# Two tiny VectorE instructions take scalar operands, and ScalarE copies the values at another point of each step

## The chip, the cores and the metric

The kernel runs on one core of a Trainium2 chip. The metric is the device time of one execution in microseconds (us), as the median of several runs. The engines are TensorE (PE, with its weight load PEld), VectorE (DVE), ScalarE (ACT), GpSimd (POOL) and SyncE (SP), which here issues DMAs.

## The reference

One perceiver layer over 8 batches of 128 tokens with 512 features, with a context of 2048 rows of 384 features for each batch. It is a cross-attention, a self-attention (softmax over the queries, causal) and a feed-forward part with rounding to small floats, each behind a layer norm:

```
x = x + _L0_xattn_ref(_layernorm(x, axis=-1), ctx_768, ...)
x = x + _L0_attn_ref(_layernorm(x, axis=-1), ...)
x = x + _L0_ffn_ref(_layernorm(x, axis=-1), ...)
```

The change concerns the cross-attention, which takes some four fifths of the time:

```
q = (x @ Wq).reshape(B, Nq, HEADS, DIM_HEAD)
k = (context @ Wk).reshape(B, context.shape[1], HEADS, DIM_HEAD)
v = (context @ Wv).reshape(B, context.shape[1], HEADS, DIM_HEAD)
sim = jnp.einsum('bihd,bjhd->bhij', q, k) * SCALE
attn = jax.nn.softmax(sim, axis=-1)
out = jnp.einsum('bhij,bjhd->bihd', attn, v)
```

## The kernel before

Every fp32 operand of a product is split into a high and a low fp16 half, and a product is made of three passes (high by high, low by high, high by low). The cross-attention is a loop over 128 slots, 16 for each batch. A slot is one head of one of four head pairs over one half of the context (1024 columns). In the first 8 slots of a batch stands the first half of the context, in the other 8 the second. `behind(s)` is true for these latter ones: there the running maximum, the sums and the weighted values of the first half are merged with the new ones.

All engines follow one hand-written schedule. Each has a function `steady(s)` that is called for s = 0 to 127, and the orders of the engines are tied together by semaphores alone. In step s:

- TensorE makes the values of slot s+1 (`value_tiles`, 18 matmuls into the one bank `v_ps`), the keys of slot s (`key_quarter`, 9 matmuls into the one bank `k_ps`), the weighted values of slot s-5 (`weighted_values`, into `o_ps`), and in even steps the scores of two slots (`scores`, 12 matmuls into `e_ps`). It may not refill `v_ps` before VectorE has made the low half of the values that stand there (`v_low`, semaphore `v_split`), nor `k_ps` before `k_low` (`k_split`), nor `e_ps` before ScalarE's second exponential of the slots there (`p_full`).
- ScalarE works three slots behind (x = s-3). `slot_bias` turns a maximum into the bias of the exponential. `exps_high` writes the exponentials in fp16 (`p_h`), `exps_full` writes them once more in fp32 and sums them (`p_f`, `p_sum`), `v_high` and `k_high` copy values and keys out of their banks as fp16, `fade_of` makes the factor by which the first half's results shrink, and `ctx_high` (every fourth step) casts a new piece of context. In an odd step x is the first slot of a pair, and both biases of the pair are made in this step.
- VectorE takes in odd steps the two maxima of the pair (`slot_maximum`, `q_max`, 128x1024 to 128x1). In slots with `behind` each is followed by `new_max`, the minimum of two columns of `q_max` (the maxima are kept negated). Then come `add_sums` (`o_den`, one column) and `accumulate` (`acc`), `o_reciprocal`, `v_low` and `k_low`.
- GpSimd makes the low half of the exponentials (`p_low`, tile `p_l`), the low half of the context (`ctx_low`, tile `ctx_l`, every fourth step, in steps 2, 6, 10 and 14 of a batch), and the normalised outputs.
- SyncE issues the DMAs that transpose `p_h` and `p_l` into `pt_h` and `pt_l`.

From slot 112 on GpSimd and VectorE also split the weights of the next stage (lines L2040 and L1578). Rows of the trace name a line: L670 is inside `three_passes`, which both the value and the key products use, L739 the scores, L759 and L761 the weighted values, L1158 `v_high`, L1166 `k_high`, L1173 `slot_bias`, L1195 `exps_high`, L1202 `exps_full`, L1523 `v_low`, L1530 `k_low`, L1537 and L1542 the two instructions of `slot_maximum`, L1554 `acc`, L1566 `o_den`, L1969 `ctx_low`.

Of the kernel before, what the change touches and what calls it, by code (L numbers as in the profile page):

```python
# [8 lines left out]
ALU = mybir.AluOpType  # L9
# [26 lines left out]
SLOTS = B * PAIRS * QUARTERS  # L36
# [24 lines left out]
def perceiver_kernel(nc, x, ctx_t, xwq, xwk, xwv, xwo, xbo, awq, abq, awk, abk, awv, abv,  # L61
# [136 lines left out]
    with ExitStack() as ctx:  # L198
# [3 lines left out]
        def sem(name):  # L202
            return ctx.enter_context(nc.semaphore(name))
# [58 lines left out]
        o_rec_ready = sem("o_rec_ready")  # L262
# [76 lines left out]
        def slot_of(s):  # L339
            return s // PER_BATCH, s % PER_BATCH // PER_HALF, s % PER_HALF // 2, s % 2  # L340
# [9 lines left out]
        def v_tiles_of(s):  # L350

            return s // PER_BATCH, s % PER_HALF // 4, s % PER_BATCH // PER_HALF * PER_HALF + 2 * (s % 4)

        def behind(s):
            return s % PER_BATCH >= PER_HALF
# [36 lines left out]
        def v_bank(s):  # L392
            return o_ps[0] if s == 1 else v_ps
# [694 lines left out]
        def _(act):  # L1088
# [29 lines left out]
            def x_norm(r):  # L1118
                act.wait_ge(rstd_ready, 3)
                act.wait_ge(shift_ready, 2)  # L1120
                act.activation(x_in[:, r, :], x_in[:, r, :], ACT.Identity, scale=rstd[:, r:r + 1],
                               bias=shift[:, r - 4:r - 3]).then_inc(xn_ready, 1)


            def x_high(r):
                act.wait_ge(xn_ready, r + 1)
                if r == 4:
                    act.wait_ge(wq_split, DCH)
                act.activation(xn_half[:, r - 4, 0, :], x_in[:, r, :], ACT.Copy).then_inc(xt_hi, 1)
# [17 lines left out]
            def v_high(s):  # L1147

                b, g, j0 = v_tiles_of(s)
                act.wait_ge(v_filled, s + 1)  # L1150
                if b and s % 4 == 0:

                    act.wait_ge(pv_done, s - PER_BATCH + 4)
                if s == PER_HALF:
                    act.wait_ge(wv_split, 2)
                elif s == PER_HALF + 4:
                    act.wait_ge(wk_split, PAIRS)
                act.activation(v[g][:, j0:j0 + 2, :, 0:DH], v_bank(s)[:, :].rearrange("p (j h d) -> p j h d", j=2, d=DH),  # L1158
                               ACT.Copy).then_inc(v_hi, 1)

            def k_high(s):
                u, i = s // 2, s % 2
                act.wait_ge(k_filled, s + 1)
                if u >= K_RING:
                    act.wait_ge(e_filled, u - K_RING + 1)
                act.activation(k_h[:, u % K_RING, i * QW:i * QW + QW], k_ps[:, :], ACT.Copy).then_inc(k_hi, 1)  # L1166

            def slot_bias(s):

                col = s % PER_BATCH  # L1170
                act.wait_ge(e_maxed, s + 1)
                top = new_max if behind(s) else q_max
                act.activation(bias[:, col:col + 1], top[:, col:col + 1], ACT.Identity, scale=EXP_SCALE, bias=SHIFT)\  # L1173
                    .then_inc(bias_ready, 1)

            def fade_of(s):

                col, old = s % PER_BATCH, s % PER_BATCH - PER_HALF
                act.wait_ge(bias_ready, s + 1)
                if s >= PER_BATCH:  # L1180
                    b, _, p, h = slot_of(s)
                    act.wait_ge(o_rec_ready, 3 * (PAIRS * (b - 1) + p) + h + 1)
                act.activation(fade[:, col:col + 1], bias[:, old:old + 1], ACT.Exp, scale=-1.0, bias=bias[:, col:col + 1])\
                    .then_inc(fade_ready, 1)

            def exps_high(s):

                col = s % PER_BATCH
                act.wait_ge(bias_ready, s + 1)
                if s == 0:  # L1190

                    act.wait_ge(xt_split, B)
                if s >= H_RING:
                    act.wait_ge(pt_h_landed[(s - H_RING) % T_RING], 16 * ((s - H_RING) // T_RING) + 16)
                act.activation(p_h[:, s % H_RING, :, :], e_ps[s % 2][:, :, :], ACT.Exp, scale=EXP_SCALE,  # L1195
                               bias=bias[:, col:col + 1]).then_inc(p_hi, 1)

            def exps_full(s):
                col = s % PER_BATCH
                if s >= F_RING:  # L1200
                    act.wait_ge(p_split, s - F_RING + 1)
                act.activation(p_f[:, s % F_RING, :, :], e_ps[s % 2][:, :, :], ACT.Exp, scale=EXP_SCALE,  # L1202
                               bias=bias[:, col:col + 1], accum_out=p_sum[:, col:col + 1]).then_inc(p_full, 1)
# [40 lines left out]
            def steady(s):  # L1244
                x = s - X_LAG
                ahead, pair = 0 <= x < SLOTS, s % 2 == 1
                if x == 0:

                    slot_bias(0)
                    v_high(s + 1)  # L1250
                    exps_high(0)
                    slot_bias(1)
                    k_high(s)
                    exps_full(0)
                    return
                if ahead:
                    if pair:
                        slot_bias(x)
                    exps_high(x)
                    if pair:  # L1260
                        slot_bias(x + 1)
                if 0 < s and s + 1 < SLOTS:
                    v_high(s + 1)
                if s == 2:
                    x_norm(7)
                    for r in (6, 7):
                        x_high(r)
                if ahead:
                    exps_full(x)
                if 0 < s < SLOTS:  # L1270
                    k_high(s)
                if ahead and behind(x):
                    fade_of(x)

            for s in range(SLOTS):
                steady(s)
                for i in QUERIES_BEHIND.get(s, ()):
                    q_high(i)
                if s == 1:
                    wv_high(1)  # L1280
                    x_norm(6)
                if s in ctx_behind:
                    ctx_high(ctx_behind[s])
                if s in load_behind:
                    load_ctx(load_behind[s])

                if 0 <= s - SLOTS + 19 < 2 * CC:
                    load_weight(s - SLOTS + 19)
                if 2 * CC <= s - SLOTS + 20 < 16:
                    load_weight(s - SLOTS + 20)  # L1290
                if s in LOAD_X:
                    load_x(LOAD_X[s])
# [67 lines left out]
            def weights_high(b, name):  # L1360
# [9 lines left out]
                else:  # L1370
# [3 lines left out]
                               scale=weight_scale(name)).then_inc(ws_hi, 1)  # L1374

            steady(SLOTS)
            slot_bias(SLOTS - 2)
            exps_high(SLOTS - 2)
# [88 lines left out]
        def _(dve):  # L1467
# [65 lines left out]
            def slot_maximum(s):  # L1533

                col, old = s % PER_BATCH, s % PER_BATCH - PER_HALF
                dve.wait_ge(e_filled, s // 2 + 1)
                ins = dve.tensor_reduce(q_max[:, col:col + 1], e_ps[s % 2][:, :, :].rearrange("p i n -> p (i n)"), AX, ALU.max,  # L1537
                                        negate=True)
                if behind(s):
                    ins.then_inc(e_reduced, 1)  # L1540
                    dve.wait_ge(e_reduced, s // PER_BATCH * PER_HALF + s % PER_HALF + 1)
                    ins = dve.tensor_tensor(new_max[:, col:col + 1], q_max[:, col:col + 1], q_max[:, old:old + 1], ALU.min)  # L1542
                ins.then_inc(e_maxed, 1)

            def accumulate(s):
# [15 lines left out]
            def add_sums(s):  # L1561
                b, _, p, h = slot_of(s)
                col, old = s % PER_BATCH, s % PER_BATCH - PER_HALF
                dve.wait_ge(p_full, s + 1)
                dve.wait_ge(fade_ready, PER_HALF * b + s % PER_HALF + 1)
                dve.scalar_tensor_tensor(o_den[:, p, h, :], p_sum[:, old:old + 1], fade[:, col:col + 1], p_sum[:, col:col + 1],  # L1566
                                         ALU.mult, ALU.add).then_inc(o_rec_ready, 1)

            def o_reciprocal(n):
                dve.wait_ge(o_rec_ready, 3 * n + 2)  # L1570
# [570 lines left out]
```

## Time and profile before

| | |
|---|---|
| median of 3 runs | 948.62 us (947.88 to 949.03) |
| the profiled execution, its own time | 949.72 us |
| its span in the trace | 947.7 us |
| granted TensorE clock, mean | 0.996 of full speed |
| TensorE busy | 908.3 us, 96% |
| VectorE busy | 600.1 us, 63% |
| ScalarE busy | 575.4 us, 61% |
| GpSimd busy | 506.7 us, 53% |

The span runs from the first to the last record of the execution, and the execution's own time is 2 us more. Busy time says how long an engine held an instruction. An instruction that waits inside the engine, after it has been started, counts as busy too. A row of the timeline gives the start, the duration, the engine, the line, the operation, what it writes and reads, how many like it are merged in the row (x3), and in brackets how long the engine had been idle before it and who released it.

### The profile page before, as it was taken

The numbers are of one execution on the slowest core, as the hardware profiler recorded it, in microseconds if no ns is written. First come the engines' busy times: TensorE is split into PE (matmuls) and PEld (weight loads), VectorE is DVE, ScalarE is ACT, GpSimd is POOL, SyncE is SP. The second block draws the span as 40 slices with busy tenths as digits, with TensorE's granted clock in tenths as the row PEclk, the third lists the DMA queues.
The fourth block names the chain that finished last, engine by engine and source line by source line (L and its number), as shares of the span: only waits on it lengthen the run. The fifth ranks groups of instructions, "written<-read, shape, count | busy, mean of one in ns | idle before, by whom it ended". The sixth has DMA issues, their size and how long they took to land.

```text
span 947.7 us, 19492 instructions
## 1 busy us (share of the span) xinstructions
PE 908.3 (96%) x7470; PEld 566.4 (60%) x7470; DVE 600.1 (63%) x973; ACT 575.4 (61%) x1014; POOL 506.7 (53%) x393
## 2 busy tenths in 40 slices
PE   6999999999999999999999999988999899999998
PEld 4556666666666666666666666655666455544444
DVE  6645665566556656665665566566866668886634
ACT  4856676666766776666677666756666522336540
POOL 4646466456545755675466556766876766310000
PEclk9999999999999999999999999999999999999999
DMA  9366566656656576565666656866798663133502
GB/s 332 89 153 149 123 136 140 154 130 134 145 123 129 129 146 132 122 138 133 123 140 154 142 123 151 186 122 129 158 183 177 113 105 96 39 107 78 178 12 79
DMA packets 340268, 126.35 MB, mean 133 GB/s; under 512 B 316113, under 2 KB 317905, under 8 KB 340177
## 3 DMA queue, kind: packets, MB, share of 16 engines
q1 hardware_dynamic: 324832, 95.87, 48.8%
q10 hardware_dynamic: 15344, 29.23, 10.3%
q8 instruction: 61, 1.00, 0.5%
q14 instruction: 31, 0.25, 0.1%
HBM read 45.36 MB, written 2.10 MB: 50 GB/s over the span
## 4 chain that ended last, share of the span: by engine, by line
PE 86%; DVE 6%; ACT 4%; issue 1%; DMA 1%; SPq 1%; POOL 0%; ACTq 0%; DVEq 0%
PE v_ps L670 26%; PE k_ps L670 24%; PE e_ps L739 9%; PE e_ps L670 8%; PE o_ps L759 5%; PE e_ps L1021 3%; PE o_ps L761 3%; DVE new_max L1542 2%; PE o_ps L776 2%; DVE q_max L1537 2%; PE o_ps L1014 1%; ACT p_h L1195 1%; PE e_ps L1014 1%; DVE v L1523 1%; ACT v L1158 1%
## 5 line engine op out<-in xcount | busy, mean ns | idle before, releaser
L1979 POOL TENSOR_TENSOR p_l<-p_f,p_h 128x1024 f16<-128x1024 f32 x128 | 273.0, 2133 | 260.7 <-ACT p_f L1202 259.9
L1537 DVE TENSOR_REDUCE q_max<-e_ps 128x1 f32<-128x1024 f32 x128 | 153.4, 1219 | 49.6 <-PE e_ps L739 49.6
L1530 DVE TENSOR_TENSOR k_l<-k_ps,k_h 128x512 f16<-128x512 f32 x128 | 88.5, 692 | 125.4 <-ACT k_h L1166 125.4
L670 PE MATMUL v_ps<-wv_h,ctx_h 128*128 128x256 f16 x756 | 124.7, 274 | 24.3 <-DVE v L1523 24.3
L1195 ACT ACTIVATE p_h<-e_ps,bias 128x1024 f16<-128x1024 f32 x128 | 143.2, 1119 | 2.4 <-issue 0.3
L1523 DVE TENSOR_TENSOR v<-v_ps,v 128x512 f16<-128x512 f32 x127 | 87.6, 690 | 88.6 <-ACT v L1158 87.9
L1202 ACT ACTIVATE p_f<-e_ps,bias 128x1024 f32<-128x1024 f32 x128 | 142.0, 1109 | 0.0
L670 PE MATMUL v_ps<-wv_l,ctx_h 128*128 128x256 f16 x756 | 124.2, 273 | 0.0
L670 PE MATMUL v_ps<-wv_h,ctx_l 128*128 128x256 f16 x756 | 124.1, 273 | 0.0
L759 PE MATMUL o_ps<-v,pt_h 128*128 128x128 f16 x1024 | 104.2, 220 | 0.6 <-DVE acc L1554 0.6
L670 PE MATMUL k_ps<-ctx_h,wk_h 128*128 128x512 f16 x384 | 104.4, 381 | 0.0
L670 PE MATMUL k_ps<-ctx_h,wk_l 128*128 128x512 f16 x384 | 103.8, 379 | 0.0
L670 PE MATMUL k_ps<-ctx_l,wk_h 128*128 128x512 f16 x384 | 103.8, 379 | 0.0
L1969 POOL TENSOR_TENSOR ctx_l<-raw,ctx_h 128x1536 f16<-128x1536 f32 x31 | 96.0, 3098 | 13.5 <-ACT ctx_h L1145 12.5
L761 PE MATMUL o_ps<-v,pt_l 128*128 128x64 f16 x1024 | 100.8, 193 | 0.0
L670 PEld LDWEIGHTS v_ps<-wv_h,ctx_h 128*128 128x128 f16 x756 | 64.7, 98 | 59.3 <-issue 52.9
L759 PEld LDWEIGHTS o_ps<-v,pt_h 128*128 128x128 f16 x1024 | 90.3, 98 | 15.7 <-issue 0.7
L1158 ACT ACTIVATE v<-v_ps 128x512 f16<-128x512 f32 x127 | 74.9, 590 | 38.8 <-PE v_ps L670 37.1
L761 PEld LDWEIGHTS o_ps<-v,pt_l 128*128 128x128 f16 x1024 | 88.6, 98 | 15.0
L1166 ACT ACTIVATE k_h<-k_ps 128x512 f16<-128x512 f32 x128 | 76.5, 598 | 16.9 <-PE k_ps L670 16.7
L670 PEld LDWEIGHTS v_ps<-wv_l,ctx_h 128*128 128x128 f16 x756 | 74.1, 98 | 8.7
L670 PEld LDWEIGHTS v_ps<-wv_h,ctx_l 128*128 128x128 f16 x756 | 74.1, 98 | 8.7
(311 smaller groups left out, 1336.9 us busy)
## 6 DMA issues: line engine op xcount, KB each, us to landing
raw<-in_ctx_t ACTq DMA_DIRECT2D x27, 768.0 KB, 5.4
w_raw<-in_w_t SPq DMA_DIRECT2D x32, 256.0 KB, 4.0
raw<-in_ctx_t SPq DMA_DIRECT2D x4, 768.0 KB, 7.3
pt_h<-p_h SPq DMA_TRANSPOSE x128, 2.9
pt_l<-p_l SPq DMA_TRANSPOSE x128, 2.8
out<-xr SPq DMA_DIRECT2D x7, 256.0 KB, 2.0
x_in<-in_x SPq DMA_DIRECT2D x6, 256.0 KB, 8.5
o_all<-in_x ACTq DMA_DIRECT2D x6, 256.0 KB, 3.7
```

Of the source, the lines that this page charges most:

```text
L670: mm = pe.matmul(acc, a(c), m(c), start=(i == 0), stop=(i == len(todo) - 1))
L739: mm = pe.matmul(e_ps[h][:, i, :], left[rows, p, tokens], right[rows, u % K_RING, cols], start=first, stop=last)
L759: pe.matmul(acc_bank[:, 0:VW], pt_h[:, s % T_RING, j, :], v[g][:, tile, head, :], start=(j == 0), stop=False, skip_group_check=True)
L761: mm = pe.matmul(acc_bank[:, 0:DH], pt_l[:, s % T_RING, j, :], v[g][:, tile, head, 0:DH], start=False, stop=(j == 2 * JT - 1), skip_group_ ...
L1158: act.activation(v[g][:, j0:j0 + 2, :, 0:DH], v_bank(s)[:, :].rearrange("p (j h d) -> p j h d", j=2, d=DH), ACT.Copy).then_inc(v_hi, 1)
L1195: act.activation(p_h[:, s % H_RING, :, :], e_ps[s % 2][:, :, :], ACT.Exp, scale=EXP_SCALE, bias=bias[:, col:col + 1]).then_inc(p_hi, 1)
L1202: act.activation(p_f[:, s % F_RING, :, :], e_ps[s % 2][:, :, :], ACT.Exp, scale=EXP_SCALE, bias=bias[:, col:col + 1], accum_out=p_sum[:, c ...
L1523: dve.tensor_tensor(v[g][:, j0:j0 + 2, :, DH:VW], v_bank(s)[:, :].rearrange("p (j h d) -> p j h d", j=2, d=DH), v[g][:, j0:j0 + 2, :, 0:DH ...
L1530: dve.tensor_tensor(k_l[:, s // 2 % K_RING, cols], k_ps[:, :], k_h[:, s // 2 % K_RING, cols], ALU.subtract)\
L1537: ins = dve.tensor_reduce(q_max[:, col:col + 1], e_ps[s % 2][:, :, :].rearrange("p i n -> p (i n)"), AX, ALU.max, negate=True)
L1969: pool.tensor_tensor(ctx_l[b % 2][:, q, :, :], raw[:, i % 2, :, :], ctx_h[b % 2][:, q, :, :], ALU.subtract).then_inc(ctx_split, 1)
L1979: pool.tensor_tensor(p_l[:, s % L_RING, :, :], p_f[:, s % F_RING, :, :], p_h[:, s % H_RING, :, :], ALU.subtract).then_inc(p_split, 1)
```

## The change

There are two parts. The first rewrites two instructions of VectorE that work on one column of 128 partitions. `new_max` was a `tensor_tensor` with two one-column tensor inputs; it becomes a `tensor_scalar` with one tensor input and one per-partition scalar operand. `o_den` was a `scalar_tensor_tensor` with two tensor inputs and a scalar; it becomes a `tensor_scalar` with one tensor input and two scalar operands. The second moves ScalarE's copy of the values, `v_high(s + 1)`: in odd steps from behind the second bias to the very front, in even steps from between the two exponentials to behind both.

```diff
                 if ahead:
-                    if pair:
-                        slot_bias(x)
-                    exps_high(x)
-                    if pair:
-                        slot_bias(x + 1)
-                if 0 < s and s + 1 < SLOTS:
-                    v_high(s + 1)
+                if ahead and not pair:
+                    exps_high(x)
                 if s == 2:
                     x_norm(7)
                     for r in (6, 7):
                         x_high(r)
-                if ahead:
+                if ahead and not pair:
+                    exps_full(x)
+                if 0 < s and s + 1 < SLOTS:
+                    v_high(s + 1)
+                if ahead and pair:
+                    slot_bias(x)
+                    exps_high(x)
+                    slot_bias(x + 1)
                     exps_full(x)
                 if 0 < s < SLOTS:
                     k_high(s)
...
-                    ins = dve.tensor_tensor(new_max[:, col:col + 1], q_max[:, col:col + 1], q_max[:, old:old + 1], ALU.min)
+                    ins = dve.tensor_scalar(new_max[:, col:col + 1], q_max[:, col:col + 1], q_max[:, old:old + 1], None, ALU.min)
...
-                dve.scalar_tensor_tensor(o_den[:, p, h, :], p_sum[:, old:old + 1], fade[:, col:col + 1], p_sum[:, col:col + 1],
-                                         ALU.mult, ALU.add).then_inc(o_rec_ready, 1)
+                dve.tensor_scalar(o_den[:, p, h, :], p_sum[:, old:old + 1], fade[:, col:col + 1], p_sum[:, col:col + 1],
+                                  ALU.mult, ALU.add).then_inc(o_rec_ready, 1)
```

ScalarE's order in one odd and the following even step of the first batch (s = 9 and 10; `bias` is `slot_bias`, `p_h` and `p_f` the two exponentials, `v_102` the values). Before:

```order
L1173 ACTIVATE bias<-q_max 128x1
L1195 ACTIVATE p_h<-e_ps,bias 128x1024
L1173 ACTIVATE bias<-q_max 128x1
L1158 ACTIVATE v_102<-v_ps 128x8x64
L1202 ACTIVATE p_f,p_sum<-e_ps,bias 128x1024
L1166 ACTIVATE k_h<-k_ps 128x512
L1195 ACTIVATE p_h<-e_ps,bias 128x1024
L1158 ACTIVATE v_102<-v_ps 128x8x64
L1202 ACTIVATE p_f,p_sum<-e_ps,bias 128x1024
L1166 ACTIVATE k_h<-k_ps 128x512
```

and with the change:

```order
L1158 ACTIVATE v_102<-v_ps 128x8x64
L1173 ACTIVATE bias<-q_max 128x1
L1195 ACTIVATE p_h<-e_ps,bias 128x1024
L1173 ACTIVATE bias<-q_max 128x1
L1202 ACTIVATE p_f,p_sum<-e_ps,bias 128x1024
L1166 ACTIVATE k_h<-k_ps 128x512
L1195 ACTIVATE p_h<-e_ps,bias 128x1024
L1202 ACTIVATE p_f,p_sum<-e_ps,bias 128x1024
L1158 ACTIVATE v_102<-v_ps 128x8x64
L1166 ACTIVATE k_h<-k_ps 128x512
```

In the odd step the values are now copied before the biases, so everything down to the copy of the keys stands one copy later behind them; in the even step the second exponential stands ahead of the copy.

In step 2 the same statement order also lets the normalisation of the last rows of x pass the copy. ScalarE before:

```order
L1145 ACTIVATE ctx_h_86<-raw 128x1536
L1158 ACTIVATE v_102<-v_ps 128x8x64
L1121 ACTIVATE x_in<-x_in,shift,rstd 128x512
L1129 ACTIVATE xn_half<-x_in 128x512 x2
L1166 ACTIVATE k_h<-k_ps 128x512
```

and with the change:

```order
L1145 ACTIVATE ctx_h_86<-raw 128x1536
L1121 ACTIVATE x_in<-x_in,shift,rstd 128x512
L1129 ACTIVATE xn_half<-x_in 128x512 x2
L1158 ACTIVATE v_102<-v_ps 128x8x64
L1166 ACTIVATE k_h<-k_ps 128x512
```

Here three small instructions moved ahead of the copy. On VectorE nothing changes its place; only the kind of the two instructions does, as in this odd step with `behind` (s = 15), before:

```order
L1537 TENSOR_REDUCE q_max<-e_ps 128x1
L1542 TENSOR_TENSOR new_max<-q_max 128x1
L1537 TENSOR_REDUCE q_max<-e_ps 128x1
L1542 TENSOR_TENSOR new_max<-q_max 128x1
L1566 SCALAR_TENSOR_TENSOR o_den<-p_sum,fade 128x1
L1554 SCALAR_TENSOR_TENSOR acc<-acc,fade,o_ps 128x128
```

and with the change:

```order
L1538 TENSOR_REDUCE q_max<-e_ps 128x1
L1543 TENSOR_SCALAR new_max<-q_max 128x1
L1538 TENSOR_REDUCE q_max<-e_ps 128x1
L1543 TENSOR_SCALAR new_max<-q_max 128x1
L1567 TENSOR_SCALAR o_den<-p_sum,fade 128x1
L1555 SCALAR_TENSOR_TENSOR acc<-acc,fade,o_ps 128x128
```

The line numbers are one higher there because the changed `steady` of ScalarE is one line longer.

## Rows read from the trace of the kernel before

**Rows 1.** The page, busy time by engine.

```profile
PE 908.3 (96%) x7470; PEld 566.4 (60%) x7470; DVE 600.1 (63%) x973; ACT 575.4 (61%) x1014; POOL 506.7 (53%) x393
```

**Rows 2.** Waits of PE: waited for, us in total, times, longest.

```profile
PE v_ps L670 <- DVE v L1523: 24.3, 17, 2.4
```

**Rows 3.** Timeline of PE, 290 to 314 us, starts of value products.

```profile
290.85 0.50 PE L670 MATMUL v_ps<-wv_h,ctx_h 128*128 128x256 f16 x3
...
297.13 0.49 PE L670 MATMUL v_ps<-wv_h,ctx_h 128*128 128x256 f16 x3 [1.52 <-DVE v L1523]
...
303.21 0.50 PE L670 MATMUL v_ps<-wv_h,ctx_h 128*128 128x256 f16 x3
...
307.81 0.49 PE L670 MATMUL v_ps<-wv_h,ctx_h 128*128 128x256 f16 x3
...
313.89 0.50 PE L670 MATMUL v_ps<-wv_h,ctx_h 128*128 128x256 f16 x3
```

**Rows 4.** Timeline of DVE, around 292 us and around 628 us.

```profile
292.21 1.99 DVE L1542 TENSOR_TENSOR new_max<-q_max 128x1 f32<-128x1 f32 x1
...
296.29 0.69 DVE L1523 TENSOR_TENSOR v<-v_ps,v 128x512 f16<-128x512 f32 x1 [0.28 <-ACT v L1158]
...
628.90 0.69 DVE L1523 TENSOR_TENSOR v<-v_ps,v 128x512 f16<-128x512 f32 x1 [0.54 <-ACT v L1158]
```

**Rows 5.** Timeline of POOL, around 291 us.

```profile
291.10 3.10 POOL L1969 TENSOR_TENSOR ctx_l<-raw,ctx_h 128x1536 f16<-128x1536 f32 x1 [0.27 <-ACT ctx_h L1145]
```

**Rows 6.** DVE instructions of L1542 and L1566: duration ns minimum/median/maximum.

```profile
L1542 DVE TENSOR_TENSOR new_max<-q_max x64: 158/160/2909, 92.1 to 749.5; 128x1 f32<-128x1 f32 x64
...
L1566 DVE SCALAR_TENSOR_TENSOR o_den<-p_sum,fade x64: 208/982/1102, 108.7 to 766.5; 128x1 f32<-128x1 f32 x64
```

**Rows 7.** Chain that ended last: value products of steps 7, 112 and 125.

```profile
69.40 2.07 PE v_ps L670 x18
...
654.46 3.17 PE v_ps L670 x18
...
726.38 2.07 PE v_ps L670 x18
```

**Rows 8.** Windows: busy time by engine, granted clock, DMA share, GB/s.

```profile
652.00:662.00 10.00, 7.56 (x56) 4.57 (x55) 5.34 (x11) 6.83 (x13) 6.13 (x7) 0.83 0.51 117
```

**Rows 9.** DVE tensor_scalar, the POOL instructions beside it, and acc.

```profile
777.00 1.15 POOL L2084 TENSOR_TENSOR n_half<-o_all,n_half 128x512 f16<-128x512 f32 x1
777.03 1.41 DVE L1652 TENSOR_SCALAR o_all<-xr,mean_var,rstd 128x512 f32<-128x512 f32 x1 [0.27 <-POOL rstd L1959]
...
797.44 1.45 POOL L2075 TENSOR_TENSOR xr<-xr,o_all 128x512 f32<-128x512 f32 x1
...
798.53 0.39 DVE L1699 TENSOR_SCALAR c_col<-c_sum,s_col 128x4 f32<-128x4 f32 x1
...
L1699 DVE TENSOR_SCALAR c_col<-c_sum,s_col x2: 229/310/390, 798.5 to 824.6; 128x4 f32<-128x4 f32 x2
```

**Rows 10.** Timeline of ACT, 309 to 319 us; DVE at 318.80.

```profile
309.97 0.60 ACT L1158 ACTIVATE v<-v_ps 128x512 f16<-128x512 f32 x1 [0.42 <-PE v_ps L670]
...
315.26 0.20 ACT L1173 ACTIVATE bias<-q_max 128x1 f32<-128x1 f32 x1 [1.20 <-DVE q_max L1537]
315.50 1.11 ACT L1195 ACTIVATE p_h<-e_ps,bias 128x1024 f16<-128x1024 f32 x1
...
316.60 0.59 ACT L1158 ACTIVATE v<-v_ps 128x512 f16<-128x512 f32 x1
317.08 1.12 ACT L1202 ACTIVATE p_f<-e_ps,bias 128x1024 f32<-128x1024 f32 x1
...
318.17 0.61 ACT L1166 ACTIVATE k_h<-k_ps 128x512 f16<-128x512 f32 x1
...
318.80 0.69 DVE L1530 TENSOR_TENSOR k_l<-k_ps,k_h 128x512 f16<-128x512 f32 x1 [0.62 <-ACT k_h L1166]
```

**Rows 11.** Timeline of PE, 303 to 310 us: keys of an even step.

```profile
309.77 0.59 PE L670 MATMUL k_ps<-ctx_h,wk_h 128*128 128x512 f16 x2
```

More of the change, by code:

```diff
@@ L1267, in steady @@
                         x_high(r)
-                if ahead:
+                if ahead and not pair:
[6 more added lines that the diff above has]
+                    slot_bias(x + 1)
                     exps_full(x)
```

## The prediction

> **What bounds the kernel now.** I read the page first: TensorE is busy for 908.3 of 947.7 us, far more than any other engine [rows 1], so only what shortens TensorE's work or its idle time (39.4 us) can count. The waits of TensorE come next. One line holds most of the idle time: 24.3 us in 17 waits of the value products on VectorE's `v_low` [rows 2]. Then the timeline of TensorE shows how regular the loop is. An odd and an even step together, a pair, take 313.89 - 303.21 = 10.68 us when nothing is late, and 303.21 - 290.85 = 12.36 us when the even step's value products wait, 1.52 us here [rows 3]. Nothing else in the loop is late: in a regular pair every engine but TensorE has idle time, and TensorE none.
>
> How much of this is there in all? From step 7 to step 125 lie 59 pairs, and the chain that ended last puts them at 726.38 - 69.40 = 656.98 us [rows 7]. At 10.68 us each they would take 630.12 us. So 26.9 us are lost in the loop. Between 652 and 662 us, behind the longest of the waits, the clock too was down: a mean of 0.83 was granted [rows 8], a mixture of 2.4 and 1.2 GHz, and one group of 18 value matmuls took 3.17 us where others take 2.07 [rows 7]. That is in the 26.9 us and goes if the wait in front of it goes.
>
> Why is `v_low` late? VectorE's order in an odd step is maximum, `new_max`, maximum, `new_max`, sums, `v_low`. `new_max` handles one column and takes 160 ns in the median, but up to 2909 [rows 6]. The one at 292.21 took 1.99 us and ended at 294.20 [rows 4]. GpSimd's `ctx_low` ran from 291.10 to 294.20 [rows 5]: the tiny instruction ended the moment the big one did. I find this in 15 of the 64 `new_max`, 14 of them behind `ctx_low` and one behind an addition of the bias row, and 15 of the 17 waits follow them (the two others lie in the opening steps). `o_den` has the same sickness, 982 ns in the median where 208 are possible [rows 6], but there `v_low` is not late behind it.
>
> Both have two tensor inputs in SBUF. That is what the Trainium skill says of such a pair (SBUF — State Buffer, Who interferes with whom): a VectorE instruction with two SBUF inputs shares a read interface with a GpSimd instruction that reads SBUF, and the later one waits for the whole of the other. By that rule, the trace agrees.
>
> **Part one, scalar operands.** After the change each has one tensor input. If that takes it out of GpSimd's way, `new_max` falls to some 0.21 us (I take the shortest `o_den`, which has a scalar operand [rows 6]) and all 15 waits go: 26.9 us, the difference to the regular pair. The other 49 become 0.05 us longer each, two in a pair, hidden: in the stalled step the whole of VectorE's chain was 1.5 us late, in a regular one `v_low` only waits for ScalarE's copy. `o_den` gives nothing, for it was on no path.
>
> No row shows a one-column `tensor_scalar` on VectorE, so the price is bounded from both sides. Lower end: free, as above, minus 26.9. Upper end: it waits as before, and part one gives 0. There are rows on the wide form. `o_all` (128x512, two scalar operands) began at 777.03, beside a GpSimd instruction that ran from 777.00 to 778.15, and took 1.41 us; `c_col` (128x4) took 390 ns and ended at 798.92 with a GpSimd instruction that ended at 798.89, while its other execution took 229 [rows 9]. So `tensor_scalar` as such isn't free of this wait. What is left is whether one column is. I think rather yes: the waiting forms stream several columns, and a single one can't be split between two paths.
>
> The Trainium skill has the rule behind the wide form (VectorE: DVE Perf Modes, Mode 2×_2P): a one-input operation that stays in SBUF is read over both ports if the outermost non-unit dimension is even; one column has no such dimension, and the text leaves it open. Read strictly the rule frees `new_max` and the sum is the same as mine; read as "equal counts are enough" it doesn't, and that is the second rival.
>
> **Part two, the order on ScalarE.** In odd steps the copy goes to the front. The values are there 309.97 - 307.81 = 2.16 us after their products begin [rows 3, 10]. From there all times are counted from the start of the odd step's value products. Copy to bias 0.48 (316.60 to 317.08), bias to `exps_high` 0.24 (315.26 to 315.50), on to `exps_full` 1.10 (315.50 to 316.60, the second bias in it), to `k_high` 1.09 (317.08 to 318.17), to `k_low` 0.63 (to 318.80), its length 0.69, and 0.15 until TensorE starts, as from the end of `v_low` at 296.98 to 297.13 [rows 3, 4, 10]. The sum is 6.54 us. TensorE wants the bank for the next keys at 309.77 - 303.21 = 6.56 us [rows 3, 11]. Before, the same chain ended at 318.80 + 0.69 + 0.15 - 313.89 = 5.75 us [rows 3, 10]. So the move eats a reserve of 0.81 us down to 0.02. This is the only place where it can hurt in every pair, and there are 61 of them: each 0.1 us beyond costs 6.1 us. I take 0.025 us a pair, 1.5 us in all. In the even step the copy of the values falls 1.4 us later, about where TensorE has its keys ready anyway; `v_low` still ends over 1 us before the next odd step needs the bank, and `exps_full`, which frees `e_ps`, starts no later than before. I cost this at nothing. If the first kind of wait stays, moving the copy does help: `v_low` no longer waits for it, 0.28 or 0.54 us in the stalled steps [rows 4].
>
> In step 2 the copy stands behind three small instructions, some 1.7 us. TensorE's step 3 starts about 1 us later, but its step 4 waited some 1.5 us for VectorE anyway (one of the two opening waits), so I count 0.2 us.
>
> **Sum.** Minus 26.9, plus 1.5, plus 0.2 is -25.2 us. The profiled execution took 949.72 us (span 947.7), 1.1 above the median of 948.62, and what is removed is the same in both. From the median: **923.4 us**.
>
> **The rivals.**
> - *Free column, but the order costs.* The chain above comes out 0.1 to 0.3 us longer than 6.54, and TensorE waits for `k_low` in each pair: 6 to 18 us, giving 928 to 940. For it: a reserve of 0.02 is less than I can read. Against: each link is measured back to back.
> - *One column waits like four.* `new_max` stretches as before, and only the copy's place helps: 15 waits shorter by 0.41 on the mean of 0.28 and 0.54, 6.2 us, less 1.7: 944.1. For it: `c_col` [rows 9]. Against: a column can't be halved.
> - *Slower.* `new_max` still waits, and the order costs over 0.10 us a pair, the point from which 61 pairs eat the 6.2 us. At 0.2 us it is 12.2 + 0.2 - 6.2 = +6.2 us, 954.8. The place is the wait of the even step's key products on `k_low`; for and against it are those of the two above together.
>
> **How the numbers follow.** Main case 0.55 (920 to 927), order costs 0.12 (928 to 940), column waits 0.20 (941 to 948), slower 0.13 (948 to 958). The range from 919 to 946 holds the first two and most of the third, a little over 0.8; the main case alone has 920 to 927. About 0.2% (1.9 us) is what a measurement of this kernel can tell from no change. Faster: 0.55 + 0.12 + 0.15 = 0.82. Same: 0.08, out of the last two. Slower: 0.10.
>
> **What would show it.** Right: no `new_max` over 0.3 us and none of the 15 waits on `v_low`; pairs of 10.68 us throughout; clock 1.00 between 620 and 670 us; `o_den` at about 0.25 us even where GpSimd runs. The order's price shows as waits of `k_ps` on `k_low`, at most 0.05 us each. The prediction is wrong if `new_max` still ends with `ctx_low`, or if new waits on `k_low` appear in most pairs.

## The result, and the profile of the changed kernel

The changed kernel takes **924.25 us** (median of 4 runs, 923.44 to 925.86), the kernel before 948.25 us on the same chip (947.32 to 949.03). The ratio is 0.9749, with a 95% interval from 0.9731 to 0.9768: faster by 24.0 us. The forecast was 923.4. The profiled execution took 923.44 us, its span is 921.5 us at a mean granted clock of 0.998.

The page of the changed kernel first: busy time by engine, and the shares of the chain that ended last.

```profile
PE 904.9 (98%) x7470; PEld 562.1 (61%) x7470; DVE 546.2 (59%) x973; ACT 565.9 (61%) x1014; POOL 508.2 (55%) x393
...
PE 93%; ACT 2%; DVE 2%; issue 1%; DMA 1%; SPq 1%; ACTq 0%; DVEq 0%
```

TensorE's busy time shrank by only 3.4 us against [rows 1]. VectorE's busy time fell by 53.9 us with not one instruction fewer: in the kernel before, at least that much of it was waiting that the trace counts as work. Next the waits of TensorE, in the columns of [rows 2].

```profile
PE v_ps L705 <- ACT ctx_h L1111: 6.7, 1, 6.7
PE e_ps L739 <- ACT p_f L1202: 2.8, 1, 2.8
PE v_ps L670 <- DVE v L1524: 1.6, 3, 0.9
PE k_ps L670 <- DVE k_l L1531: 0.6, 1, 0.6
```

The line with 24.3 us in 17 waits [rows 2] is down to 1.6 in 3, all in the opening. The wait of the keys on `k_low`, which the new order on ScalarE could have brought in each of 61 pairs, is there once, behind step 125. Two VectorE instructions, as in [rows 6] (shortest, median and longest in ns):

```profile
L1543 DVE TENSOR_SCALAR new_max<-q_max x64: 212/214/216, 91.8 to 722.7; 128x1 f32<-128x1 f32 x64
```

```profile
L1567 DVE TENSOR_SCALAR o_den<-p_sum,fade x64: 257/265/269, 107.4 to 740.0; 128x1 f32<-128x1 f32 x64
```

The longest of 64 `new_max` is 216 ns, where it was 2909; 28 of the 64 lie wholly within a `ctx_low`. The timeline around one of the places that used to stall (start, duration, engine, line, instruction, idle time before it):

```profile
282.95 3.09 POOL L1970 TENSOR_TENSOR ctx_l<-raw,ctx_h 128x1536 f16<-128x1536 f32 x1 [0.76 <-ACT ctx_h L1145]
...
284.07 0.21 DVE L1543 TENSOR_SCALAR new_max<-q_max 128x1 f32<-128x1 f32 x1
...
286.09 0.67 DVE L1524 TENSOR_TENSOR v<-v_ps,v 128x512 f16<-128x512 f32 x1
...
287.30 0.49 PE L670 MATMUL v_ps<-wv_h,ctx_h 128*128 128x256 f16 x3
```

`ctx_low` runs from 282.95 to 286.04, `new_max` starts in its middle, at 284.07, and is done at 284.28. TensorE starts the even step's value products with no wait in front. `v_low` starts at 286.09 and ends at 286.76, 0.54 us ahead of them. The pair here lasts as long as any other, as the starts of the odd steps' value products show; the row of the keys is that of the even step.

```profile
282.70 0.50 PE L670 MATMUL v_ps<-wv_h,ctx_h 128*128 128x256 f16 x3
...
289.26 0.81 PE L670 MATMUL k_ps<-ctx_h,wk_h 128*128 128x512 f16 x3
...
293.38 0.50 PE L670 MATMUL v_ps<-wv_h,ctx_h 128*128 128x256 f16 x3
...
304.07 0.50 PE L670 MATMUL v_ps<-wv_h,ctx_h 128*128 128x256 f16 x3
```

Where the 26.2 us between the two spans lie can be read from the chain that ended last:

```profile
69.12 2.07 PE v_ps L670 x18
...
699.38 2.08 PE v_ps L670 x18
```

The 59 pairs from step 7 to step 125 take 699.38 - 69.12 = 630.26 us, where they took 656.98 [rows 7]: minus 26.72. The opening up to step 7 is 0.28 us shorter, the stretch behind step 125 0.80 us longer (222.12 for 221.32). The sum is -26.2 us. The clock, 0.83 between 652 and 662 us in [rows 8], is full in the same window and around it (columns as in [rows 8]):

```profile
620.00:670.00 50.00, 50.00 (x457) 33.01 (x455) 32.67 (x61) 32.40 (x61) 42.59 (x36) 1.00 0.81 167
652.00:662.00 10.00, 10.00 (x94) 6.49 (x93) 6.81 (x13) 5.98 (x12) 8.49 (x9) 1.00 0.85 185
```

### The profile page after: what moved, and what is told of

It reads as the page before. It is cut to its first block, busy times and chain, and to the rows that moved or that the text cites. A ratio compares the mean times of both kernels' runs of the same rounds, so it can differ in the third digit from the quotient of the medians.

```text
span 921.5 us, 19492 instructions
## 1 busy us (share of the span) xinstructions
PE 904.9 (98%) x7470; PEld 562.1 (61%) x7470; DVE 546.2 (59%) x973; ACT 565.9 (61%) x1014; POOL 508.2 (55%) x393
## 4 chain that ended last, share of the span: by engine, by line
PE 93%; ACT 2%; DVE 2%; issue 1%; DMA 1%; SPq 1%; ACTq 0%; DVEq 0%
PE v_ps L670 28%; PE k_ps L670 26%; PE e_ps L739 10%; PE e_ps L670 8%; PE o_ps L759 6%; PE o_ps L761 3%; PE e_ps L1021 3%; PE o_ps L776 2%; PE o_ps L1014 1%; PE e_ps L1014 1%; PE o_ps L954 1%; PE v_ps L1014 1%; SPq L636 1%; DMA raw<-in_ctx_t 1%; DVE q_max L1538 0%
## 5 line engine op out<-in xcount | busy, mean ns | idle before, releaser
L1158 ACT ACTIVATE v<-v_ps 128x512 f16<-128x512 f32 x127 | 77.1, 607 | 173.6 <-PE v_ps L670 171.5
```

## The experiments

**1. Only the scalar operands.** Both edits on VectorE, and ScalarE's order of the kernel before.

```diff
-                    ins = dve.tensor_tensor(new_max[:, col:col + 1], q_max[:, col:col + 1], q_max[:, old:old + 1], ALU.min)
+                    ins = dve.tensor_scalar(new_max[:, col:col + 1], q_max[:, col:col + 1], q_max[:, old:old + 1], None, ALU.min)
...
-                dve.scalar_tensor_tensor(o_den[:, p, h, :], p_sum[:, old:old + 1], fade[:, col:col + 1], p_sum[:, col:col + 1],
-                                         ALU.mult, ALU.add).then_inc(o_rec_ready, 1)
+                dve.tensor_scalar(o_den[:, p, h, :], p_sum[:, old:old + 1], fade[:, col:col + 1], p_sum[:, col:col + 1],
+                                  ALU.mult, ALU.add).then_inc(o_rec_ready, 1)
```

> Part one alone: scalar operands for new_max and o_den, ScalarE's order as before. My theory (the gain is all from new_max, the new order costs next to nothing): 922 to 925 us, ratio to before about 0.973, the waits of TensorE on v_low gone and the reserve of the keys' chain back at 0.8 us. Rival (the new order is needed, since v_low otherwise waits for a copy that stands behind the bias): 928 to 935 us.

Measured: 923.75 us (922.74 to 924.66, 5 runs), ratio 0.9724 with an interval from 0.9709 to 0.9740. That is all of the gain. From the chain: steps 7 to 125 take 699.58 - 69.32 = 630.26 us, to the hundredth what they take in the changed kernel. So in these two executions the new order on ScalarE adds nothing to the loop and costs it nothing, once `new_max` is free.

**2. Only the new order on ScalarE.** Against the changed kernel, both instructions on VectorE are those of before.

```diff
-                    ins = dve.tensor_scalar(new_max[:, col:col + 1], q_max[:, col:col + 1], q_max[:, old:old + 1], None, ALU.min)
+                    ins = dve.tensor_tensor(new_max[:, col:col + 1], q_max[:, col:col + 1], q_max[:, old:old + 1], ALU.min)
...
```

> Part two alone: the new order on ScalarE, new_max and o_den with two tensor inputs as before. My theory: new_max still ends with GpSimd's instruction in 15 places, each wait of TensorE is 0.28 or 0.54 us shorter, 943 to 946 us. Rival (the order does more, because v_low no longer stands behind the late bias at all): below 938 us. Rival (the order costs in every pair): 948 us or more.

Measured: 940.78 us (940.11 to 943.29, 6 runs), ratio 0.9909 (0.9895 to 0.9924), some 8.6 us under the kernel before and some 2 us below the 943 to 946 that I had expected. The waits are still there, but shorter; the waits of TensorE in this run:

```profile
PE v_ps L670 <- DVE v L1524: 15.3, 17, 1.6
```

And its timeline at the stretch that corresponds to [rows 4]:

```profile
289.76 1.99 DVE L1543 TENSOR_TENSOR new_max<-q_max 128x1 f32<-128x1 f32 x1
...
293.39 0.16 DVE L1572 RECIPROCAL o_rec<-o_den 128x2 f32<-128x2 f32 x1
293.47 0.67 DVE L1524 TENSOR_TENSOR v<-v_ps,v 128x512 f16<-128x512 f32 x1
...
294.29 0.49 PE L670 MATMUL v_ps<-wv_h,ctx_h 128*128 128x256 f16 x3 [1.13 <-DVE v L1524]
```

`new_max` is held for 1.99 us as before, but `v_low` now follows the instruction ahead of it without a gap, and TensorE waits 1.13 us in place of 1.52 [rows 3]. The same holds at all six places of this kind; at the six of the other kind the wait is 0.70 in place of 1.34 us. Of the other three, 2.44, 0.60 and 2.44 us long, 1.12 and 1.56 are left, and between 652 and 662 us the clock is full.

**3. Only `new_max` as `tensor_scalar`.** Against the first experiment, `o_den` is that of before.

```diff
-                dve.tensor_scalar(o_den[:, p, h, :], p_sum[:, old:old + 1], fade[:, col:col + 1], p_sum[:, col:col + 1],
-                                  ALU.mult, ALU.add).then_inc(o_rec_ready, 1)
+                dve.scalar_tensor_tensor(o_den[:, p, h, :], p_sum[:, old:old + 1], fade[:, col:col + 1], p_sum[:, col:col + 1],
+                                         ALU.mult, ALU.add).then_inc(o_rec_ready, 1)
```

> Only new_max gets a scalar operand; o_den keeps two tensor inputs and the order is that of before. My theory (o_den is on no path): the same time as with both, 922 to 925 us, although o_den still takes up to 1.1 us. Rival (a stretched o_den in odd steps makes v_low late once new_max is short): waits of TensorE of 0.1 to 0.3 us behind it, 926 us or more.

Measured: 923.88 us (922.95 to 924.62, 4 runs), ratio 0.9728 (0.9713 to 0.9742). That can't be told from the first experiment: one line of one instruction is the whole gain, as far as times can tell. `o_den` still took 745 ns on the mean, and it cost nothing but in one place, which the trace shows:

```profile
626.09 3.10 POOL L1969 TENSOR_TENSOR ctx_l<-raw,ctx_h 128x1536 f16<-128x1536 f32 x1
...
627.81 1.40 DVE L1566 SCALAR_TENSOR_TENSOR o_den<-p_sum,fade 128x1 f32<-128x1 f32 x1
...
630.27 0.49 PE L670 MATMUL v_ps<-wv_h,ctx_h 128*128 128x256 f16 x3 [0.58 <-DVE v L1523]
```

With `new_max` out of the way it is now `o_den` that `ctx_low` holds, to 629.21, beside `ctx_low`'s own end at 629.19. `v_low` comes late, and TensorE waits 0.58 us. Steps 7 to 125 take 700.51 - 69.52 = 630.99 us, 0.73 more than in the first experiment. The rival was right in this one place.

**4 and 5. `new_max` with two and with three columns.** Still a `tensor_scalar` with the same scalar operand, but over the neighbouring columns of `q_max` too, into a tile with room for them; ScalarE reads only the column that it needs. What is computed beside it is not used. With two columns:

```diff
-        ("q_max", [P, PER_BATCH], F32), ("bias", [P, PER_BATCH], F32), ("new_max", [P, PER_BATCH], F32),
+        ("q_max", [P, PER_BATCH], F32), ("bias", [P, PER_BATCH], F32), ("new_max", [P, PER_BATCH, 2], F32),
...
-                    ins = dve.tensor_scalar(new_max[:, col:col + 1], q_max[:, col:col + 1], q_max[:, old:old + 1], None, ALU.min)
+                    ins = dve.tensor_scalar(new_max[:, col, :], q_max[:, col - 1:col + 1], q_max[:, old:old + 1], None, ALU.min)
...
```

> The changed kernel, with new_max over two columns in place of one (the second is not used), everything else the same. If one column is free because a single column can't be divided, two will wait for GpSimd as the 128x4 c_col did: new_max up to 2.9 us, 942 to 947 us. Rival (any tensor_scalar of a few columns is free, and c_col's 390 ns had another reason): new_max at 0.22 us throughout, 923 to 925 us.

> The changed kernel with new_max over three columns (two unused). Two columns waited for GpSimd (941.7 us, new_max up to 2.43 us). If what frees one column is that it can't be divided, three wait as two do: 940 to 943 us. Rival (an odd number of columns is free): 923 to 925 us and new_max at 0.22 us throughout.

Measured: 941.70 us (941.48 to 942.48, 4 runs), ratio 0.9917 (0.9902 to 0.9932), with two columns, and 941.91 us (940.79 to 943.63, 4 runs), ratio 0.9914 (0.9888 to 0.9941), with three. Both are the time of the second experiment, in which `new_max` is a `tensor_tensor`. The longest of each, first of the kernel with two columns, then of the one with three:

```profile
L1543 DVE TENSOR_SCALAR new_max<-q_max x64: 228/229/2432, 91.9 to 741.0; 128x2 f32<-128x2 f32 x64
```

```profile
L1543 DVE TENSOR_SCALAR new_max<-q_max x64: 228/229/2423, 92.2 to 740.8; 128x3 f32<-128x3 f32 x64
```

And one of them with `ctx_low` beside it, in the kernel with three columns:

```profile
113.34 3.10 POOL L1970 TENSOR_TENSOR ctx_l<-raw,ctx_h 128x1536 f16<-128x1536 f32 x1 [0.77 <-ACT ctx_h L1145]
114.46 2.00 DVE L1543 TENSOR_SCALAR new_max<-q_max 128x3 f32<-128x3 f32 x1
```

Both end within 0.02 us of 116.45. So it isn't the scalar operand by itself that frees `new_max`: a second column brings the wait back, for 15 ns of additional work. An odd number of columns doesn't help either. That the hardware divides such an instruction between two ways to the memory, and can't divide one column, fits all three counts, but it is inferred from them and not seen.

**6. One more small instruction on ScalarE.** Against the changed kernel, in the odd steps ahead of the first bias, to see how much reserve the new order leaves.

```diff
+                    act.activation(spare[:, :], ident[:, 0:1], ACT.Copy)
```

> The changed kernel with one more tiny ScalarE instruction (one column, into a tile that nobody reads) between the copy of the values and the first bias of each odd step. My theory (the keys' chain has a reserve of 0.02 us): each of some 61 pairs gets longer by the length that the instruction adds to the chain, about 0.1 us, so 929 to 932 us and waits of the key products on k_low in most pairs. Rival (there is more reserve than I worked out): no change, 924 us.

Measured: 929.49 us (928.60 to 930.84, 4 runs), ratio 0.9784 (0.9755 to 0.9813), 5.2 us over the changed kernel's median, and 5.1 over the same kernel on the same chip (experiment 8). Rows of its timeline, ScalarE's small instruction, `k_low` and TensorE's keys of the even step:

```profile
284.54 0.50 PE L670 MATMUL v_ps<-wv_h,ctx_h 128*128 128x256 f16 x3
...
287.20 0.20 ACT L1267 ACTIVATE spare<-ident 128x1 f32<-128x1 f32 x1
287.30 0.19 ACT L1173 ACTIVATE bias<-new_max 128x1 f32<-128x1 f32 x1
...
290.34 0.69 DVE L1532 TENSOR_TENSOR k_l<-k_ps,k_h 128x512 f16<-128x512 f32 x1 [1.75 <-ACT k_h L1166]
...
291.18 0.81 PE L670 MATMUL k_ps<-ctx_h,wk_h 128*128 128x512 f16 x3
```

The bias follows the added instruction by 0.10 us (287.20 to 287.30). `k_low` starts 290.34 - 284.54 = 5.80 us into the pair, 0.08 later than in the changed kernel, and the keys start 291.18 - 284.54 = 6.64 us into it, 0.08 later too. All of `k_low`'s delay reaches TensorE, so the order has no reserve left that these rows can show, where the sum of links gave 0.02 us. Steps 7 to 125 take 705.06 - 69.39 = 635.67 us, or 5.41 more: 59 times 0.08 are 4.7, and one wait of 0.63 us at 692.04, for nothing that the profile shows, stands in them too. Each 0.1 us beyond the reserve does cost some 6 us. The waits of the keys on `k_low` that I had expected in most pairs are not listed as waits (there is one, of 0.5 us, behind step 125); the delay shows only in the starts, 10.76 us a pair for 10.68.

**7. The opening as before.** Against the changed kernel, the copy of step 2 goes back behind the three small instructions.

```diff
-                if s == 2:
-                    x_norm(7)
-                    for r in (6, 7):
-                        x_high(r)
...
+                if s == 2:
+                    x_norm(7)
+                    for r in (6, 7):
+                        x_high(r)
```

(The lines stand ahead of `exps_full` in the changed kernel, and behind the values' copy here.)

> The changed kernel, but in step 2 the copy of the values stands ahead of the three small instructions as before. My theory (the later copy made one opening wait of 0.9 us and took 1.0 us off the next): the same time as the changed kernel within 0.5 us. Rival (the opening costs what the trace shows as the new wait): 0.9 us less.

Measured: 925.77 us (925.16 to 926.07, 4 runs), ratio 0.9742 (0.9719 to 0.9765). The interval of the ratio overlaps that of the changed kernel, so the two can't be told apart by it. Still, each of the four runs is above each of the four of the changed kernel on the same chip (experiment 8), 1.4 us by the medians, where I had expected 0.5 at most. By the chains step 7 starts at 69.58 us here, and at 69.12 and 68.81 in two executions of the changed kernel. Whether the new opening is worth that much stays open.

**8. The changed kernel again**, unchanged, beside other kernels.

> The changed kernel once more, beside the others on the same chip: 924 us, a ratio of 0.974 to before.

Measured: 924.35 us (922.36 to 924.76, 4 runs), ratio 0.9724 (0.9699 to 0.9749), the ratio of the first experiment. What is left between runs of one kernel is about 0.25% of the ratio, so the order's price in all can't be bounded better than to some 2 us by times. The chains bound it better in the pairs, which take 10.68 us here as well, but not in all: steps 7 to 125 take 700.55 - 68.81 = 631.74 us, 1.48 more than in the first profile. Most of it is one wait of 1.33 us in front of weighted values, which that profile doesn't have:

```profile
698.31 0.22 PE L759 MATMUL o_ps<-v,pt_h 128*128 128x128 f16 x1 [1.33 <-issue]
```

One of 1.48 us is in the seventh experiment, of 0.93 in the fourth and of 0.63 in the sixth, all four with the new order, and none in the first, third and tenth, which have the old one. But the changed kernel's first profile and the second and fifth experiments have the new order and no such wait. So it may belong to the order in some executions; no run here settles it.

**9. `ctx_low` one step later.** In the kernel before, GpSimd's large instruction goes from the place where it lies over `new_max` to behind `p_low` of the next odd step.

```diff
-                if s in ctx_behind:
+                if s in ctx_behind and s < 6:
...
+                if s >= 7 and s - 1 in ctx_behind:
+                    ctx_low(ctx_behind[s - 1])
```

> The kernel before, new_max with two tensor inputs, but GpSimd makes the low half of the context one step later (behind p_low of the next odd step). If it is GpSimd's instruction that holds new_max, the waits move with it: the 14 behind ctx_low vanish in the pairs where they were, and new ones appear only where the displaced p_low now ends late, in the pair behind step 15 of each batch, some 7 of them. So about half of the 26.9 us goes: 933 to 940 us. Rival (new_max is slow in those pairs for a reason of its own, such as the transposing DMAs): the same 15 waits in the same steps, 948 us.

Measured: 1086.07 us (1083.96 to 1086.87, 4 runs), ratio 1.1416 (1.1394 to 1.1437). This missed by more than 100 us, through something that I had not followed. The waits, of TensorE and of ScalarE:

```profile
PE e_ps L739 <- ACT p_f L1202: 118.8, 27, 5.7
...
PE v_ps L670 <- DVE v L1523: 4.8, 4, 1.9
```

```profile
ACT p_h L1195 <- POOL ctx_l L1969: 145.6, 24, 7.0
```

ScalarE issues the transfer of the next context block in its own order, and that transfer must wait until `ctx_low` has read the old one. With `ctx_low` late, ScalarE stood there for 145.6 us in 24 waits with its exponentials queued behind. The waits on `v_low` did fall, to 4.8 us in 4, two of them in the opening, but in a schedule so different that this proves little. The kernel doesn't answer the question that it was made for.

**10. The first `fold` ahead of the last scores.** Against the first experiment, to use the 2.8 us that TensorE waits for ScalarE's `p_f` behind the loop.

```diff
-            scores(UNITS - 1)
             fold(0)
+            scores(UNITS - 1)
```

> Scalar operands with the order of before, and the first product of the weights of the next stage (fold 0) put ahead of the last scores, where TensorE waits 2.8 us for an exponential and its clock then falls. If that product fills the wait: 2 to 5 us below the scalar-operand kernel, 919 to 922 us. Rival (the last scores, the exponentials behind them and everything that hangs on these just come later): 923 to 925 us.

Measured: 921.85 us (920.66 to 923.00, 5 runs), ratio 0.9693 (0.9675 to 0.9710). It is the fastest kernel of the study, ahead of both kernels, and its interval only just touches that of the first experiment. The wait on `p_f` falls from 2.8 to 0.23 us, in the first row, but a new one of 1.97 us on VectorE's `f_l` stands behind it, in the second. The medians differ by 1.9 us, on two chips, more than the difference of these waits. The clock bears on the rest: in the first experiment it was 0.83 between 710 and 720 us and again between 720 and 730, here 1.00 and 0.83. How much of the rest that is I leave open.

```profile
717.68 0.39 PE L739 MATMUL e_ps<-k_h,q_h 64*128 64x512 f16 x2 [0.23 <-ACT p_f L1202]
...
724.50 0.38 PE L670 MATMUL v_ps<-wo_h,q_h 128*128 128x512 f16 x1 [1.97 <-DVE f_l L1666]
```

**11. `ctx_low` and the transfer behind it later.** The ninth again, with ScalarE's issue of the next block moved too.

```diff
-                load_behind[QUARTERS * n + 3] = EARLY_CTX + 1 + n
+                load_behind[QUARTERS * n + 5] = EARLY_CTX + 1 + n
```

> The kernel before, with GpSimd's ctx_low one step later, and ScalarE's loading of the next context block moved behind it as well, from step 4n+3 to step 4n+5, so that ScalarE no longer waits in order for GpSimd ahead of its exponentials (what held it for 145.6 us in the run with ctx_low alone moved). new_max is still the two-pointerless tensor_tensor of 128x1. Theory (new_max is held by whichever GpSimd instruction runs at that moment, nothing else): the 15 waits of value products on v_low at the old places vanish or fall under 0.5 us each, new_max is long only where a GpSimd instruction still lies over it, some 7 places in the pair behind step 15 of each batch; 933 to 940 us. Rival (the long new_max belongs to the step, whatever GpSimd does): the same 15 waits, 24 us in them, 948 us. If ScalarE's waits for ctx_low come back in another place, over 960 us and the run tells nothing of either.

Measured: 934.87 us (934.10 to 935.77, 4 runs), ratio 0.9842 (0.9819 to 0.9864). No instruction of VectorE differs from the kernel before, and 14.8 us are gone. Of the waits on `v_low` 12.4 us in 10 are left, two of them in the opening (1.52 and 0.16). The long `new_max` are gone from the regular places, and there are new ones in the pair of steps 17 and 18 and each 16 steps on, seven in all; the eighth wait, 1.86 us at 628.98, lies where GpSimd has the added work of the late slots. The timeline of one of the seven:

```profile
294.10 3.10 POOL L1969 TENSOR_TENSOR ctx_l<-raw,ctx_h 128x1536 f16<-128x1536 f32 x1
...
297.16 2.12 POOL L1979 TENSOR_TENSOR p_l<-p_f,p_h 128x1024 f16<-128x1024 f32 x1
297.56 1.74 DVE L1542 TENSOR_TENSOR new_max<-q_max 128x1 f32<-128x1 f32 x1
```

`ctx_low` is over at 297.20, but it has pushed `p_low` back, which now runs from 297.16 to 299.28, and `new_max`, begun at 297.56, ends at 299.30. So there is nothing special in `ctx_low`: `p_low` holds `new_max` to its end just so. TensorE waits 1.26 us behind each of these seven. Moving GpSimd's work thus brings less than taking `new_max` out of its way.

## Why the prediction was right, point by point

**What bounds the kernel.** Right. The loss in the loop was put at 26.9 us, and 26.72 came back. The pairs take 10.68 us throughout, and the clock is full where it was 0.83 [rows 8].

**The cause of the late `v_low`.** Right, and now shown by changing each side of it: VectorE's instruction alone (experiment 3) brings the whole gain, and GpSimd's schedule (experiment 11, with ScalarE's issue of a transfer behind it) moves the waits to where GpSimd's work went.

**One column is free.** This was the open point, argued from "a single one can't be split", with 0.20 for the rival that it waits like four. Right by the third, fourth and fifth experiments: one column never over 216 ns, two columns up to 2432, three up to 2423. The Trainium skill says it in one more place than I had used (Advanced Engine Details and Errata, VectorE Performance Modes): the mode that reads over both ports wants the outermost non-unit dimensions of source and destination even, or odd, above one and equal, and VectorE and GpSimd block each other there. The trace agrees at all three counts.

**`new_max` in the free case.** I took 0.21 us from the shortest `o_den`; it is 0.214. `o_den` was put at nothing, "for it was on no path". That held for the kernel before, and nearly so with `new_max` freed: experiment 3 has one wait of 0.58 us behind a held `o_den`, too little for the times to show.

**The order's chain, 6.54 us against 6.56.** The rows of the chain in the changed kernel, ScalarE and VectorE, counted from 282.70:

```profile
284.88 0.60 ACT L1158 ACTIVATE v<-v_ps 128x512 f16<-128x512 f32 x1 [2.00 <-PE v_ps L670]
...
285.37 0.20 ACT L1173 ACTIVATE bias<-new_max 128x1 f32<-128x1 f32 x1
...
287.79 0.59 ACT L1166 ACTIVATE k_h<-k_ps 128x512 f16<-128x512 f32 x1
...
288.42 0.69 DVE L1531 TENSOR_TENSOR k_l<-k_ps,k_h 128x512 f16<-128x512 f32 x1 [1.66 <-ACT k_h L1166]
```

The value copy starts 2.18 us in (I had 2.16), the first bias 2.67, `k_high` 5.09, `k_low` 5.72, and 5.72 + 0.69 + 0.15 = 6.56 us, exactly when TensorE wants the bank. The forecast sum was 0.02 us short, and the reserve is nil to the hundredth that can be read, as experiment 6 confirms. The price I put on it, 0.025 us a pair and 1.5 us in all, was too high: the pairs take 10.68 us, and the loop 630.26 us, with the new order and with the old one (experiment 8 has what this leaves open). The rival "the order costs" would have needed 0.1 us more, and experiment 6 shows what then happens, at the rate I had given.

**The copy's place if the waits stay.** The mechanism was right and the size off. I put the term at 6.2 us, less 1.7, so 4.5; experiment 2 gave 8.6, and its chain shows 646.83 us for the 59 pairs, 10.2 under [rows 7]. I had read how long `v_low` stood idle for the copy, 0.28 and 0.54 us [rows 4]. TensorE's waits fell by 0.39 and 0.64 instead, because `v_low` can start before the instruction ahead of it has ended (at 293.47, with the other lasting to 293.55), so that it goes earlier than the idle time tells; it was also 0.02 us shorter. And I had taken the two longest waits for ordinary ones: they fell by 1.3 and 0.9 us. All in all 6 x (0.39 + 0.64) + 1.32 + 0.60 + 0.88 = 9.0 us of waiting went, and the slow clock, which I had not counted here, went as well. The second rival is therefore faster than the 944.1 that I gave: experiments 4 and 5 took 941.7 and 941.9 us, 7.6 and 9.0 under the kernel before on their chips.

**The opening, +0.2 us.** Too small to be told: step 7 is reached 0.28 us earlier, but two executions of the changed kernel differ by 0.31 there (69.12 and 68.81). Beside one of 0.16, the two waits in it are now 0.91 and 0.55 us, where there was one of 1.53. As reasoned, what is lost in step 3 is given back in step 4.

**Behind step 125.** Not in the prediction: that stretch is 0.80 us longer, with the one wait of 0.6 us on `k_low` in it. The same kind of hold makes this wait:

```profile
708.41 1.62 DVE L1579 SCALAR_TENSOR_TENSOR wo_l<-raw,wo_h 128x512 f16<-128x512 f32 x1
...
709.96 0.68 DVE L1531 TENSOR_TENSOR k_l<-k_ps,k_h 128x512 f16<-128x512 f32 x1
```

`wo_l`, also with two tensor inputs, takes 1.62 us where most of its kind take 0.68, beside a `p_low` that ends at 709.49, and `k_low` stands behind it. With the old order it starts at 707.51, ahead of `p_low`, and takes 0.68 (first experiment). But there the stretch is 922.3 - 699.58 = 222.72 us, longer still. So not all of it is a matter of the order, and I leave it open.

**The sum.** The forecast of 923.4 lies closer to the 924.25 than its terms deserve. By the spans the change took off 26.2 us, by the medians 24.0, for the profiled execution of the kernel before was slower than its median and that of the changed kernel the fastest of four. The forecast of -25.2 lies between: it had 1.5 us for the order that the loop did not pay, and nothing for the 0.80 behind step 125. That the forecast came out within 1 us of the median is therefore luck; that the 26.9 of the loop came back is not.

**What did the change's second part bring?** With the first part in place, nothing that shows. It is worth 8.6 us where `new_max` still waits. The two parts don't add up: 0.9724 and 0.9909 alone, and together 0.9749 and, measured again, 0.9724.

## What to carry to other kernels

A very short VectorE instruction whose longest execution is many times its median, as `new_max` here, may be waiting, and the timeline tells for whom: look at what ends at the same moment on GpSimd. Where both its inputs are single columns, give one of them as a scalar operand, and keep the tensor operand at one column, not two. A reserve in a chain that TensorE waits for could be worked out here link by link to 0.02 us, but a wait's gain is to be read from start to start, not from the idle time beside the waiting instruction; and before moving a large instruction on one engine, look for what another engine issues in order behind it.

## What the runs showed of the hardware that I had not expected

A `tensor_scalar` on 128x1 runs beside a GpSimd `tensor_tensor` unhindered: 212 to 216 ns in 64 executions, 28 of them within a `ctx_low`. With a second or third column it is held up to 2432 and 2423 ns. The work itself grows from 214 to 229 ns only. Where nothing holds it, the form with a scalar operand is the slower one: 214 ns in the median for 160 of `new_max` as `tensor_tensor`, and 257 for 208, each the shortest, of `o_den` with one scalar operand less.
